# A Perceiver layer on one core: the query projection from one float32 pass to three float32r passes

## The reference

```python
x = x + xattn(_layernorm(x), ctx_1024, ctx_1024, Wq, bq, Wk, bk, Wv, bv)     # sigmoid weights over 25088 rows
# attention, 16 heads of 32, latents of 128, causal
h = _layernorm(x)
c_kv = h @ W_kv_down
k_rope = _rotary_apply(c_kv @ W_k_rope, cos, sin)
k = (c_kv @ W_k_up).reshape(Bb, Tt, NH, HD)
v = (c_kv @ W_v_up).reshape(Bb, Tt, NH, HD)
q = (h @ W_q).reshape(Bb, Tt, NH, HD)                                        # 512 x 512: the projection of this case
q_rope = _rotary_apply(h @ W_q_rope, cos, sin)
scores = einsum('bqhd,bkhd->bhqk', q, k) + einsum('bqr,bkr->bqk', q_rope, k_rope)[:, None]
w = softmax(causal(scores / sqrt(64)))
x = x + einsum('bhqk,bkhd->bqhd', w, v).reshape(Bb, Tt, 512) @ W_o
x = x + ffn(_layernorm(x), gate_w, wg, wu, wd)                               # 8 experts, one for each row
```

## Time and profile before

| what | us |
|---|---|
| median of 3 runs | 579.70 |
| the profiled execution | 579.98 |
| its span | 578.2 |
| TensorE busy, whole span | 569.3 |
| TensorE / VectorE / ScalarE busy, 490 to 502 us | 11.48 / 9.21 / 5.81 |
| TensorE / VectorE / ScalarE busy, 502 to 510 us | 7.58 / 7.17 / 4.75 |
| GpSimd busy, whole span | 1.7, all before 2.2 us |

### The profile page before, as it was taken

One profiled execution on the slowest core, in us unless ns is written; L12 is line 12 of the kernel. 1 busy time (PEld: TensorE's weight loads), 2 busy tenths in 40 slices (PEclk: granted clock), 3 DMA queues, 4 the chain that ended last, 5 costly groups with the idle time before them and its releaser, 6 DMA issues.

```text
span 578.2 us, 7983 instructions
## 1 busy us (share of the span) xinstructions
PE 569.3 (98%) x2986; PEld 477.0 (82%) x2986; DVE 456.6 (79%) x509; ACT 398.1 (69%) x533; POOL 1.7 (0%) x7
## 2 busy tenths in 40 slices
PE   8999999999999999999999999999999999999998
PEld 4788888888888888888888888888888887867887
DVE  4987878787878798889888988787878787888742
ACT  4876777767767787777777877776767674587321
POOL 1000000000000000000000000000000000000000
PEclk9999999999999999999999999999999999999999
DMA  8568787867677877788778787768586744000201
GB/s 328 203 201 244 234 239 236 238 207 250 207 218 255 256 253 228 246 253 253 228 252 257 247 240 238 217 219 233 204 247 192 239 150 191 1 2 2 73 1 37
DMA packets 33238, 115.89 MB, mean 200 GB/s; under 512 B 4080, under 2 KB 4784, under 8 KB 32944
## 3 DMA queue, kind: packets, MB, share of 16 engines
q1 hardware_dynamic: 32768, 115.05, 62.8%
q10 hardware_dynamic: 432, 0.33, 0.2%
HBM read 114.84 MB, written 0.52 MB: 200 GB/s over the span
## 4 chain that ended last, share of the span: by engine, by line
PE 94%; DVE 3%; ACT 2%; DMA 1%; issue 1%; ACTq 0%
PE ps L384 46%; PE ps L328 23%; PE ps L346 12%; PE ps L862 4%; PE ps L894 2%; PE ps L751 1%; PE ps L491 1%; PE ps L557 1%; ACT w L680 1%; PE ps L658 1%; DMA x_s<-in_x 1%; PE ps L467 1%; PE ps L687 1%; DVE st L507 0%; DVE x_s L506 0%
## 5 line engine op out<-in xcount | busy, mean ns | idle before, releaser
L384 PE MATMUL ps<-nh,zl 128*128 128x512 f32 x392 | 144.2, 389 | 0.0
L384 PE MATMUL ps<-nh,zh 128*128 128x512 f32 x392 | 144.2, 389 | 0.0
L384 PE MATMUL ps<-nl,zh 128*128 128x512 f32 x392 | 144.1, 389 | 0.0
L361 DVE TENSOR_TENSOR zl<-zf,zh 128x1024 fp32r<-128x1024 f32 x49 | 60.1, 1226 | 78.3 <-ACT zh L360 78.3
L247 DVE TENSOR_TENSOR nl<-rawn,nh 128x1024 fp32r<-128x1024 f32 x97 | 115.5, 1220 | 4.7 <-issue 3.0
L244 ACT ACTIVATE nh<-rawn 128x1024 fp32r<-128x1024 f32 x97 | 101.4, 1058 | 19.0 <-DMA rawn<-in_ctxn 18.4
L233 DVE TENSOR_TENSOR tl<-rawt,th 128x1024 fp32r<-128x1024 f32 x96 | 112.8, 1216 | 0.0
L228 ACT ACTIVATE th<-rawt 128x1024 fp32r<-128x1024 f32 x96 | 96.2, 1051 | 0.6 <-DMA rawt<-in_ctxt 0.4
L356 ACT ACTIVATE zf<-ps 128x512 f32<-128x512 f32 x98 | 58.3, 597 | 49.7 <-PE ps L346 43.8
L384 PEld LDWEIGHTS ps<-nh,zl 128*128 128x128 f32 x392 | 73.5, 188 | 15.7 <-DVE zl L361 0.5
L384 PEld LDWEIGHTS ps<-nl,zh 128*128 128x128 f32 x392 | 73.6, 188 | 15.3
(11 more groups left out here) (177 smaller groups left out, 602.3 us busy)
## 6 DMA issues: line engine op xcount, KB each, us to landing
rawn<-in_ctxn SPq DMA_DIRECT2D x97, 512.0 KB, 6.7
rawt<-in_ctxt SPq DMA_DIRECT2D x96, 512.0 KB, 4.9
h_s<-in_wg SPq DMA_DIRECT2D x4, 512.0 KB, 7.4
h_s<-in_wu SPq DMA_DIRECT2D x4, 512.0 KB, 7.2
wds<-in_wd SPq DMA_DIRECT2D x4, 512.0 KB, 5.2
raw<-in_ctxt SPq DMA_DIRECT2D x2, 512.0 KB, 7.6
h_s<-in_wvt SPq DMA_DIRECT2D x2, 512.0 KB, 7.5
wq_s<-in_wq SPq DMA_DIRECT2D x1, 1024.0 KB, 5.2
```

Of the source, the lines that this page charges most:

```text
L361: ZL[b] = put("vector", lambda e: e.tensor_tensor(zl[b % 2][:], zf[:], zh[b % 2][:], ALU.subtract), [ZH[b]] + av, "zl")
L384: AV[b] = put("tensor", lambda e, z=z, n=n, i=i, j=j, r=r: e.matmul(bank(4 + r), z[:, j * T + r * P:j * T + r * P + P], n[:, j * D:(j + 1) ...
```

## The change

The projection's weights and rows are split into a high and a low part as elsewhere. New tiles are wqh and wql (the weights), hqh and hql (the rows; the order calls them hq0 and hq1). ScalarE copies the high parts; the low parts are subtractions on GpSimd (elsewhere in the kernel VectorE does them). The weights and the rows of half 0 are split right behind the second `wol`, the rows of half 1 (`split_h(1)`) behind the table load for the exponentials. `query` now takes a list of blocks and does for each 12 matmuls of float32r: high weights x high rows, low weights x high rows, high weights x low rows; for blocks 0 and 1 the first two passes of both come before the third of both.

```diff
@@ -151,13 +151,16 @@
         proj = ExitStack()
         wq_s = proj.enter_context(nc.sbuf_tensor("wq_s", [P, 4, D], F32))
         proj.close()
+        wql = once("wql", [P, 4, D], F32R)
         hTh = sb("hTh", [P, 4, T], F32R)
         hTl = sb("hTl", [P, 4, T], F32R)
         wo_s = once("wo_s", [P, 4, D])
         wol = sb("wol", [P, 4, D], F32R)
         woh = sb("woh", [P, 4, D], F32R)
         wds = [sb(f"wds{i}", [P, 1024]) for i in range(2)]
+        wqh = once("wqh", [P, 4, D], F32R)
         wdh = sb("wdh", [P, 8, D], F32R)
+        hqh, hql = several("hq", 2, [P, 4, T], F32R)
         wdl = sb("wdl", [P, 8, D], F32R)
         esum = sb("esum", [P, 2, 16])
         einv = sb("einv", [P, 2, 16])
@@ -549,6 +552,22 @@
         YT.append(sum_turned(1, 7, m))
         HT = [put("vector", lambda e: e.tensor_scalar(hT[:, :, half(0)], chunks(0), 2.0, None, ALU.mult), [n], "lne_v")]
         WOL = low_o[1]()
+        WQH, WQL, HQH, HQL = [], [], [], []
+        for k in range(2):
+            n = slice(2 * k, 2 * k + 2)
+            WQH.append(put("scalar", lambda e, n=n: e.activation(flat(wqh[:, n]), flat(wq_s[:, n]), ACT.Copy),
+                           [DWQ2, DONE[1]], "wqh"))
+            WQL.append(put("gpsimd", lambda e, n=n: e.tensor_tensor(flat(wql[:, n]), flat(wq_s[:, n]), flat(wqh[:, n]),
+                                                                    ALU.subtract), [WQH[k]], "wql"))
+
+        def split_h(r):
+            n = half(r)
+            ready = HT[r] if isinstance(HT[r], list) else [HT[r]]
+            HQH.append(put("scalar", lambda e: e.activation(hqh[:, :, n], hT[:, :, n], ACT.Copy), ready, "hqh"))
+            HQL.append(put("gpsimd", lambda e: e.tensor_tensor(hql[:, :, n], hT[:, :, n], hqh[:, :, n], ALU.subtract),
+                           [HQH[r]], "hql"))
+
+        split_h(0)
         XM.append(project_v(1, 3, []))
 
 
@@ -609,8 +628,17 @@
                     done.append(put("scalar", lambda e, b=b, d=d: e.activation(d, b, ACT.Copy), [mark], "qaa"))
             QA[g] = done
 
-        def query(t, o, wait):
-            return project(o, lambda c: wq_s[:, c, P * t:P * t + P], slice(0, T), wait, "q")
+        def query(ts, outs, wait):
+            steps = [(wqh, hqh, HQH + WQH), (wql, hqh, WQL), (wqh, hql, HQL)]
+            turns = [(i, k) for i in range(2) for k in range(len(ts))] if len(ts) > 1 else [(0, 0), (1, 0)]
+            for i, k in turns + [(2, k) for k in range(len(ts))]:
+                w, h, ready = steps[i]
+                n = slice(P * ts[k], P * ts[k] + P)
+                for c in range(4):
+                    m = put("tensor", lambda e, w=w, h=h, c=c, i=i, k=k, n=n: e.matmul(
+                        outs[k], w[:, c, n], h[:, c, :], start=(i == 0 and k == 0 and c == 0), stop=((i, k, c) == (2, len(ts) - 1, 3))),
+                        [*ready, *wait], "q" if (i, k, c) == (2, len(ts) - 1, 3) else None)
+            return m
 
         latents(0, 1, 2, 4, 6, [])
         X1[1], RS[1] = norm_stats(1, 3, [XM[1]])
@@ -627,14 +655,14 @@
         table(ACT.Exp)
         KT0 = turned(1, 0, 1, KR[0])
         spread(1, 0, ka, KT0)
+        split_h(1)
         k_copies(1, 3)
-        query(0, bank(1)[:, 0:T], [KT0, HT[1], DWQ2])
-        QT = query(1, bank(1)[:, T:2 * T], [])
+        QT = query([0, 1], [bank(1)[:, 0:T], bank(1)[:, T:2 * T]], [KT0, HT[1], DWQ2])
         spread(0, 1, qa, turned(0, 1, 7, QR[1]))
         f = turned(1, 1, 5, KR[1])
         q_copies(0, QT, bank(1).rearrange("p (t n) -> p t n", t=2), lambda i: slice(i // 2, 4, 2))
         spread(1, 1, ka, f)
-        QT = query(2, bank(2)[:, 0:T], [ROT[0, 0]])
+        QT = query([2], [bank(2)[:, 0:T]], [ROT[0, 0]])
         VE[1] = put("scalar", lambda e: e.activation(v_s[:, 1, :], bank(0), ACT.Copy), [VT[1]], "ve_a")
 
 
@@ -769,7 +797,7 @@
         a_scores(0)
         maxima(0)
         q_copies(1, QT, bank(2)[:, 0:T], lambda i: 4 + i // 2)
-        QT = query(3, bank(1)[:, 0:T], QA[0])
+        QT = query([3], [bank(1)[:, 0:T]], QA[0])
         exps(0)
         q_copies(1, QT, bank(1)[:, 0:T], lambda i: 6 + i // 2)
         a_scores(1)
```

## The result

The changed kernel has a median of 582.85 us in 6 runs (582.56 to 583.93), the kernel before 579.76 us in 6 runs on the same chip (579.69 to 580.26): a ratio of 1.0053, with a 95% interval of 1.0043 to 1.0063. It is slower by 3.1 us, where 2.7 us were forecast.

The account below looks back on a forecast made before the run. The prediction took VectorE's full queue in the tail, not TensorE, to set the first scores. Delays of 1.0 + 0.7 + 1.0 = 2.7 us on 579.98 gave 582.7, or 582.4 us as a median; range 579.4 to 584.6.

Parts of the forecast that it names:

- VectorE's queue sets the scores, not the projection: Before the first scores, 498.02 to 508.08 us: VectorE's full queue sets their start, so TensorE's 1.5 us saving gains nothing.
- the chain as printed: The before profile's chain of waits, naming TensorE's query projection (3.47 us to 506.27) ahead of the scores at 508.40.
- ScalarE's copies are free: High-part copies on ScalarE fall in idle time or delay key copies 0.4 us harmlessly; cost nothing, 0.4 us if cover fails.
- GpSimd's price: Time per GpSimd subtraction, taken as twice the memset: 1.9 us for 1024 columns, 1.04 us for 512.
- The turns: In the tail, VectorE and GpSimd exclude each other at SBUF for whole instructions; 2.7 us on the path, chance 0.64.
- the first two terms: Second half's normalisation on VectorE: x_s late by 1.0 us behind wol, then the small L516 held up 0.7 us more.
- The third term: Rows' last GpSimd subtraction goes in between two L593 copies on VectorE, making the second wait 1.04 us; counted as 1.0.
- the signs in the prediction: Expected after: wol and first subtraction collide, h_s 1 to 2.5 us later, an L593 or L588 long near the last subtraction.
- Side by side: Rival: GpSimd and VectorE hardly hold each other up, under 1.2 us in all; 579.5 to 580.5 us, chance 0.28.
- projection on the path: Rival: scores follow the query projection, so TensorE's 0.6 and 0.4 us come off; 578.4 to 579.1 us, chance 0.05.
- GpSimd far slower: Rival: 1024-column subtractions take 5.8 us or more, so TensorE waits for wql; 583 us and more at 8 us, chance 0.03.

Follow-up runs that it names:

- the kernel without GpSimd: The changed kernel with its four GpSimd subtractions removed, low-part passes reading the high parts; 579.87 us, ratio 0.9995.
- writes alone: The changed kernel with each GpSimd subtraction replaced by two memsets of the same tile, so GpSimd reads nothing; 580.13 us, ratio 1.0.
- splits alone: The changed kernel with the query projection in float32 from wq_s again, all splits kept but unused; 582.96 us, ratio 1.0049.
- the rows' part alone: The changed kernel with the weights' GpSimd subtractions removed and the rows' kept, the weights' low pass reading the high part; 581.38 us, ratio 1.002.
- the kernel with the filled gap: The changed kernel plus ten float32r matmuls into an unused bank while TensorE waits for h_s of the second half; 583.22 us, ratio 1.0055.

## Why the prediction was right, and where it wasn't

*VectorE's queue sets the scores, not the projection.* Right, against the chain as printed: shorter passes alone gave nothing (579.87 against 580.0), and giving the old projection back lost nothing (582.96 against 582.85). The passes themselves were sized well: 2.89 us on the chain after for blocks 0 and 1, where 2.86 was worked out. (Behind the projection the chain has four ScalarE pieces up to 508.40, not three; nothing rests on it.)

*ScalarE's copies are free.* Right: they are all in the kernel without GpSimd, which took 579.87 us.

*GpSimd's price.* Too low: 1.9 and 1.04 us were taken, between bounds of 1.21 to 2.85 and 0.69 to 1.56; measured were 2.35 to 2.40 for 1024 columns and 1.26 to 1.30 for 512 where nothing held them up. By the estimate that the prediction drew from the Trainium skill (GPSIMD Engine Reference, section 3.1), 2.25 and 1.1 us, the sum was 583.7 us in the profiled execution's measure; the durations agree better with it than with the value taken.

*The turns.* Right, and shown by the pair of runs with writes alone and with splits alone. The first two terms came out as 1.28 and 1.03 us for 1.0 and 0.7, by the longer subtractions.

*The third term.* This is the step that failed: "the second copy waits 1.04 us" was 0.33 us on another instruction, an L588 of the kernel before, which the signs in the prediction allowed for and the sum did not. The forecast let TensorE keep its clock through a wait that it had itself made longer: with x_s and L519 late by 2.3 us, TensorE stood idle for 2.36 us, ran the latents at 1.2 GHz, and so moved the last subtraction from the copies to a short sum, and the projection so far back that VectorE waited 0.37 us for it. With TensorE kept busy the copies paid 0.98 us, close to the 1.04 of the forecast. That the loss agreed to 0.4 us (3.1 against 2.7) is partly luck: the third term's -0.7 and the unforeseen wait's +0.4 stand against the first two terms' +0.6.

*The rivals.* Side by side is excluded by wol's 3.28 us beside the subtractions and 1.22 without them, projection on the path by the kernel without GpSimd, whose passes are as short and whose time is that of before. GpSimd far slower: the wql passes follow the first ones without a wait, at 507.22, so no.

*What stays open.* When the clock falls. The idle 2.36 us of TensorE, read in one profiled execution of each kernel, went with a mean clock of 0.997 in all six executions of the change, but in only two of four with the old projection. The wait of 2.28 us went with the lower clock in six of ten with the rows' part alone, one of 2.27 us, before the scores of the kernel with the filled gap, in none of four. The kernel before shows 0.997 too, in 3 of its 52 executions beside these runs, which took 581.03 to 581.18 us, about 1.1 us longer than its median; none of them was profiled. What decides this the runs don't show.

## What to carry to other kernels

Work that is put on an idle engine isn't free because the engine is idle: ask which instructions of the path read the same memory. In these runs each instruction of VectorE with two inputs from SBUF waited for the rest of a GpSimd instruction that reads SBUF, however small it was itself, and copies from SBUF to SBUF did too. Look for such a cost in durations, not in waits. And if a term lengthens an idle time of TensorE, work out the terms behind it at both levels of its clock.

## What the runs showed of the hardware that wasn't expected

- The hold-up doesn't go by the size of what is held up: an instruction on 128x1 numbers, 0.22 us long, took 1.25 us. Beside running subtractions, instructions with one input from SBUF kept their times: the reciprocal at 497.04 (0.16 us), x_s with its other input from PSUM (0.68 us), and L605 at 505.67 (0.28 us), also with its other input from PSUM and of the shape of the L607 behind it, which has two inputs from SBUF and took 0.61 us.
- Two GpSimd subtractions in a row let VectorE in between them: wol's record ends at 495.03, 1.08 us behind the first subtraction's end, and the second subtraction's record of 3.36 us, 1.0 us more than the 2.36 of one that nothing held up, holds that time.
- GpSimd needs 1.9 to 2.0 times what VectorE needs for the same subtraction (2.35 to 2.40 us against 1.22).
- One float32 pass of 256 columns takes 0.22 us (24 in 5.34), and a matmul is two of them; a float32r one takes 0.12 to 0.13 us (24 in 2.89, 36 in 4.65). Three float32r passes save 0.06 us a matmul of this shape (5.34 less 4.65, over 12), before any split is paid.
